# A macaron block on one core: first products of batches 2 to 5 moved from the loop to the front, the front's order changed, and the turn of xa put inside a value tile

## Chip, core and metric

The kernel runs on one core of a Trainium2 chip. The metric is the device time of one execution in microseconds (us), the median of several runs.

## What is computed

x has 8 batches of 512 tokens with 256 channels. All is float32. The first and the last stage are the same small FFN: eight adapters out of 32 are summed with weights into one 256 x 256 matrix. Between them stands a block with a recurrence over time (wkv) and a channel mix with 1024 hidden channels.

```python
def _L0_ffn_ref(x, W, b, ids, weights):
    out = jnp.einsum('k,kod,bsd->bso', weights, W[ids], x)
    return out + jnp.einsum('k,ko->o', weights, b[ids])

x = x + 0.5 * _L0_ffn_ref(_layernorm(x), ...)          # x1
x = x + _L0_attn_ref(_layernorm(x), ...)               # below
x = x + 0.5 * _L0_ffn_ref(_layernorm(x), ...)

# _L0_attn_ref
h = layernorm(x, ln1_g, ln1_b); hh = time_shift(h)
xk = h * tm_k + hh * (1 - tm_k)                        # xv, xr alike
k = xk @ Wk.T; v = xv @ Wv.T; sr = sigmoid(xr @ Wr.T)
x = x + (sr * wkv(time_decay, time_first, k, v)) @ Wo.T
h = layernorm(x, ln2_g, ln2_b); hh = time_shift(h)
xk = h * cm_k + hh * (1 - cm_k)                        # xr alike
kk = square(relu(xk @ Wck.T))
return x + sigmoid(xr @ Wcr.T) * (kk @ Wcv.T)
```

## The kernel before

Each of the engines (TensorE, VectorE, ScalarE, GpSimd, and SyncE for the transfers) has its own list of instructions, written out by hand. It works through its list in order and waits at semaphores for the others. Every batch passes through the stages below. Tiles lie with the tokens on the partitions (x1, xa, xs: 4 tiles of 128 tokens, 256 channels) or with the channels on the partitions (h1, xk, kk: 512 tokens in the free direction).

1. First product, y1 (L293, L271): `xt` (the batch of x, loaded with its channels on the partitions) times `ffn_t`, 16 matmuls in two banks of PSUM. The layer norm is applied behind it: VectorE takes the statistics of x (`stats_x`), GpSimd the inverse root `rstd_x` (L966) and adds the bias to x (`bias_to_x`, L986), and VectorE forms x1 = y1 * rstd_x + x (`add_first`, L696).
2. VectorE normalises x1 (`norm_first`, L716). TensorE turns it (`turn_x1`), ScalarE scales it into h1 (L473). VectorE forms the difference of h1 (L725) and the mixes xk, xv, xr (L734).
3. TensorE: products k, v, r (`front_k`, `front_v`, `front_r`, L277). VectorE scans and forms the gated wkv (L742 to L792), with exponentials on ScalarE and GpSimd. TensorE: output product (L326, L271).
4. VectorE adds it to xa (`add_output`, L798), takes statistics; GpSimd: inverse root `rstd_xa`; VectorE normalises (`norm_output`, L810). GpSimd sums xs = x1 + xa (`attention_sum`, L1016). TensorE turns xa (`turn_xa`), ScalarE forms h2 and the first part of the mix; VectorE finishes the mix xck (L818). ScalarE rounds it to its high part `xck_hi` (L503), VectorE takes the rest, `xck_lo` (L832).
5. TensorE: eight key blocks of the hidden layer, with the high and low parts of operand and weight (`channel_keys`, L340, L341, L344), a gate product (`channel_gate`), and four value tiles (`channel_values`, L362). ScalarE squares the relus. VectorE adds the values (`value_sum`, L840 and L843); GpSimd adds the bias of the last FFN (x2b, L986).
6. TensorE turns xs and makes the second product, and VectorE adds it (`add_second`, L866) for the store.

The lists are software pipelined. First comes a front for batch 0 (and the sums of batch 1). Then step e of a loop runs stages 5 and 6 of batch e and e - 1, stages 2 to 4 of batch f = e + 1, and stage 1 of batch f + 1. On TensorE a step is: keys with the turns of x1 and of xs between them, k, v, three keys, r, second product, gate, value tile 0, output product, first half of y1, value tile 1, second half of y1, turn of xa, value tiles 2 and 3. The next step begins with the keys, which want `xck_hi` and `xck_lo` of batch f.

PSUM is four pairs of banks. `PAIR` says which stage uses which pair, and `take` makes TensorE wait until the pair's last user has been read. In the front, TensorE runs matmuls on the identity (`warm(p, n)`, L254) that nobody reads, in its waits. `xt` has two buffers, x1 three. The SP queue loads in its own order: `load_x` (L199), `load_xt` (L206) and `store` (L213); a load into a buffer in use waits for its reader.

Of the kernel before, what the change touches and what calls it, by code (L numbers as in the profile page):

```python
# [10 lines left out]
P = 128  # L11
# [8 lines left out]
def build(nc, x, xt, ffn_w, ffn_b, ids, gates, vectors, wk, wv, wr, wo, wcr, wck, wcv, out):  # L20
# [4 lines left out]
    CH = C // P  # L25
# [6 lines left out]
    LAST = B - 1  # L32

    with ExitStack() as ctx:  # L34
# [38 lines left out]
        x2b = sb("x2b", [P, NT, C])  # L73
        kinds = ("x", "x1", "xa", "x2")
# [58 lines left out]
        thc_done, kvs_done = sem("thc_done"), sem("kvs_done")  # L133
# [33 lines left out]
        PAIR_BUT = {("y1", 1): 1, ("turn_x2", LAST): 2, ("y2", LAST): 1}  # L167
# [25 lines left out]
        def _(sp):  # L193
# [27 lines left out]
            load_xt(0)  # L221
            load_xt(1)
            load_x(1)
# [9 lines left out]
            load_xt(3)  # L233
            for e in range(B):
                load_x(e + 3)
                store(e - 1)
                load_xt(e + 4)
# [5 lines left out]
        def _(pe):  # L243
# [21 lines left out]
            def to_tokens(stage, src, w, signal, b, filled, part=range(BANKS)):  # L265
                for i in part:
                    take(pair_of(stage, b), i, signal, 2 * b + i + 1)
# [12 lines left out]
            def ffn_setup():  # L280
                pe.wait_ge(s_const, 4)
                warm(3, 36)
# [8 lines left out]
                last.then_inc(s_ffn_ps, 1)  # L291

            def first_product(f, part=range(BANKS)):  # L293
# [3 lines left out]
                to_tokens("y1", xt_sb[f % 2], ffn_t, x1_done, f, y1_ps, part)  # L297
# [55 lines left out]
            def channel_values(e, t):  # L353
# [3 lines left out]
                if t % TB == 0:  # L357
                    take(PAIR["kv"], i, kvs_done, 2 * e + i + 1)
                for n in range(HB):
# [4 lines left out]
                if t % TB == TB - 1:  # L364
                    last.then_inc(kv_ps, 1)
# [26 lines left out]
            warm(3, 8)  # L392
# [3 lines left out]
            pe.wait_ge(q_done, 2)  # L396
            warm(2, 47)
            output_product(0)
            pe.wait_ge(t1_done, 2)
            warm(3, 14)  # L400
            turn_xa(0)
            warm(3, 11)
            for e in range(B):
                f = e + 1

                early = (0, 1, 2) if has(e - 1) else (0, 1, 2, 3)
                late = (5, 6, 7) if has(e - 1) else (6, 7)
                channel_keys(e, early)
                if has(f):
                    turn_x1(f)  # L410
                if has(e - 1):
                    channel_keys(e, (3,))
                    turn_x2(e - 1)
                    channel_keys(e, (4,))
                else:
                    channel_keys(e, (4, 5))
# [3 lines left out]
                channel_keys(e, late)  # L420
# [8 lines left out]
                if has(f + 1):  # L429
                    first_product(f + 1, (0,))  # L430
                channel_values(e, 1)
                if has(f + 1):
                    first_product(f + 1, (1,))
                if has(f):
                    turn_xa(f)
                channel_values(e, 2)
# [657 lines left out]
```

## Time and profile before

| what | us |
|---|---|
| median of 3 runs (469.83 to 472.84) | 470.56 |
| the profiled execution, its own time | 470.55 |
| its span, first to last instruction | 468.8 |
| TensorE matmul busy in the span | 449.7 (96%) |
| VectorE busy | 385.6 (82%) |
| ScalarE busy | 255.4 (54%) |
| GpSimd busy | 156.3 (33%) |
| mean granted TensorE clock | 0.991 of full |

In the names of the profile PE is TensorE's matmul, PEld its weight load, DVE is VectorE, ACT ScalarE, POOL GpSimd and SP SyncE. A row of the timeline begins with the start and the length of a merged group of instructions; in brackets stands how long the engine had been idle ahead of it, and which instruction ended that. Buffer numbers are left out of the names: x is x1 there, and `work` is any tile of the recurrence. A busy PE is not a PE at its peak, since the ends of matmuls are modelled. The matmuls of the front include the ones on the identity.

### The profile page before, as it was taken

The page shows a single profiled execution, that of the slowest core. Times are in us where ns is not written, and L with a number is a line of the kernel's source. Part 1 is how long each engine was busy: PE and PEld are TensorE (multiplying, and loading weights), DVE is VectorE, ACT ScalarE, POOL GpSimd, SP SyncE. Part 2 cuts the span into 40 slices and gives each one's busy share as a digit, 9 for nine tenths or more (in the row PEclk, how much of TensorE's full clock was granted, in tenths as well). Part 3 has the DMA queues.
Part 4 walks back from the last instruction along what each step waited for, and adds up shares of the span by engine and source line. Part 5 has one row for each costly group of instructions (what it writes and reads, how often), then busy time and mean ns, then how long its engine had stood idle before and what let it go on. Part 6 is the DMA issues. An engine that isn't in the chain of part 4 may idle for free. (4 is left out here: it accounts for less than half of the span.)

```text
span 468.8 us, 5983 instructions
## 1 busy us (share of the span) xinstructions
PE 449.7 (96%) x2034; PEld 353.1 (75%) x2034; DVE 385.6 (82%) x796; ACT 255.4 (54%) x415; POOL 156.3 (33%) x126
## 2 busy tenths in 40 slices
PE   8959979999999999999999999999999999999996
PEld 8734966488857886788758886788668885778884
DVE  3778987998999798989899899979898999967124
ACT  1136637772878067924786167824794287816500
POOL 1344042415440543236240644035232444023010
PEclk9989999999999999999999999999999999999999
DMA  6950001002000020012001110010001000000101
GB/s 210 373 205 1 1 7 39 0 2 89 0 1 15 33 90 0 1 45 91 0 0 47 39 52 0 0 47 0 1 0 47 0 1 1 17 30 0 45 1 45
DMA packets 15952, 18.49 MB, mean 39 GB/s; under 512 B 1066, under 2 KB 13618, under 8 KB 15922
## 3 DMA queue, kind: packets, MB, share of 16 engines
q1 hardware_dynamic: 14522, 17.05, 10.4%
q10 hardware_dynamic: 1400, 1.07, 0.8%
q8 instruction: 16, 0.26, 0.2%
q14 instruction: 14, 0.11, 0.1%
HBM read 13.92 MB, written 4.19 MB: 39 GB/s over the span
## 5 line engine op out<-in xcount | busy, mean ns | idle before, releaser
L362 PE MATMUL pair<-wcv_sb,kk 128*128 128x256 f32 x512 | 114.3, 379 | 0.0
L362 PEld LDWEIGHTS pair<-wcv_sb,kk 128*128 128x128 f32 x512 | 96.7, 190 | 12.8
L966 POOL TENSOR_TENSOR rstd_x<-vare_x,nhalf 128x4 f32<-128x4 f32 (+1 forms) x25 | 30.2, 1207 | 102.0 <-DVE vare_x L654 101.1
L481 ACT ACTIVATE h<-pair,vec 128x512 f32<-128x512 f32 x16 | 11.6, 775 | 89.6 <-PE pair L262 89.6
L340 PE MATMUL pair<-xck_hi,wck_hi 128*128 128x512 f32 x128 | 55.6, 434 | 2.4 <-ACT xck_hi L503 1.3
L344 PE MATMUL pair<-xck_lo,wck_hi 128*128 128x512 f32 x128 | 50.2, 392 | 0.0
L341 PE MATMUL pair<-xck_hi,wck_lo 128*128 128x512 f32 x128 | 50.0, 390 | 0.0
L522 ACT ACTIVATE kk<-pair 128x512 f32<-128x512 f32 x64 | 37.9, 592 | 15.4 <-PE pair L344 13.5
L1009 POOL TENSOR_SCALAR work<-work,lowest 128x512 f32<-128x512 f32 x16 | 26.6, 1664 | 54.8 <-DVE work L745 54.8
L526 ACT ACTIVATE kk<-kk 128x512 f32<-128x512 f32 x64 | 38.8, 634 | 0.8
L986 POOL TENSOR_TENSOR x2b<-xs,bias_bc 128x512 f32<-128x512 f32 x15 | 19.2, 1280 | 52.1 <-DVE xs L843 52.1
L277 PE MATMUL pair<-xk,wk_sb 128*128 128x512 f32 x64 | 31.7, 642 | 4.3 <-issue 3.9
L340 PEld LDWEIGHTS pair<-xck_hi,wck_hi 128*128 128x128 f32 x128 | 24.1, 188 | 9.2 <-issue 3.2
L254 PE MATMUL pair<-ident 128*128 128x128 f32 x232 | 28.9, 288 | 2.1 <-POOL h L961 2.1
L254 PEld LDWEIGHTS pair<-ident 128*128 128x128 f32 x232 | 28.6, 205 | 2.7 <-POOL h L961 2.1
L271 PE MATMUL pair<-ffn_t,xt 128*128 128x256 f32 x128 | 29.9, 380 | 0.7 <-ACT ffn_t L458 0.7
L271 PE MATMUL pair<-ffn_t,x2t 128*128 128x256 f32 x128 | 29.2, 380 | 0.7 <-ACT x2t L552 0.7
L271 PEld LDWEIGHTS pair<-ffn_t,x2t 128*128 128x128 f32 x128 | 24.2, 190 | 6.8 <-issue 2.9
L277 PE MATMUL pair<-xr,wr_sb 128*128 128x512 f32 x64 | 28.8, 593 | 0.5 <-DVE xr L734 0.5
L271 PE MATMUL pair<-wo_sb,rwkv 128*128 128x256 f32 x128 | 29.1, 380 | 0.1
L271 PE MATMUL pair<-wcr_sb,xcr 128*128 128x256 f32 x128 | 28.9, 379 | 0.0
L277 PE MATMUL pair<-xv,wv_sb 128*128 128x512 f32 x64 | 28.8, 592 | 0.0
(115 smaller groups left out, 876.8 us busy)
## 6 DMA issues: line engine op xcount, KB each, us to landing
x<-in_x_dram SPq DMA_DIRECT2D x8, 512.0 KB, 4.7
xt<-in_xt_dram SPq DMA_DIRECT2D x8, 512.0 KB, 5.1
out_dram<-xs SPq DMA_DIRECT2D x16, 256.0 KB, 2.1
work<-in_ffn_w_dram ACTq DMA_DIRECT2D x4, 256.0 KB, 4.5
work<-in_ffn_w_dram SPq DMA_DIRECT2D x4, 256.0 KB, 4.6
kk<-in_wck_dram SPq DMA_DIRECT2D x1, 1024.0 KB, 9.0
wcv_sb<-in_wcv_dram SPq DMA_DIRECT2D x1, 1024.0 KB, 10.4
wk_sb<-in_wk_dram SPq DMA_DIRECT2D x1, 256.0 KB, 8.4
```

The costliest lines, as they stand in the source:

```text
L254: nc.tensor.matmul(pair[p][:, 0, 0:P], ident[:, :], ident[:, :], start=True, stop=True)
L271: last = nc.tensor.matmul(bank_of(stage, b, i)[:, t * C:(t + 1) * C], src[:, h, tok:tok + P], w[:, h, :], start=h == 0, stop=h == CH - 1)
L277: last = nc.tensor.matmul(bank, w[:, h, o * P:(o + 1) * P], src[:, h, :], start=h == 0, stop=h == CH - 1)
L340: nc.tensor.matmul(key_bank(n), wck_hi[:, h, cols], xck_hi[:, h, :], start=h == 0, stop=False)
L341: nc.tensor.matmul(key_bank(n), wck_lo[:, h, cols], xck_hi[:, h, :], start=False, stop=False)
L344: last = nc.tensor.matmul(key_bank(n), wck_hi[:, h, cols], xck_lo[:, h, :], start=False, stop=h == CH - 1)
L362: last = nc.tensor.matmul(bank_of("kv", e, i)[:, t % TB * C:(t % TB + 1) * C], kk[:, n, tok:tok + P], wcv_sb[:, n, :], start=n == 0, stop= ...
L522: nc.scalar.activation(kk[:, n, :], key_bank(n), ACT.Relu).then_inc(relu_done, 1)
L526: nc.scalar.activation(kk[:, n, :], kk[:, n, :], ACT.Square).then_inc(sq_done, 1)
L966: nc.gpsimd.tensor_tensor(dst, src, power, ALU.pow).then_inc(done, 1)
L986: nc.gpsimd.tensor_tensor(dst, tile, bias_bc[:, :].rearrange("p (a c) -> p a c", a=1).broadcast_to([P, tiles, C]), ALU.add).then_inc(done, 1)
L1009: nc.gpsimd.tensor_scalar(e_v[:, h, 0:T], q[:, h, 0:T], lowest[:, h:h + 1], None, ALU.max).then_inc(held_done, 1)
```

## The change

The first products of batches 2, 3, 4 and 5 (`EARLY`) leave the steps 0 to 3 and are computed in the front: 2 and 3 behind the r product of batch 0, 4 behind its output product, 5 behind its turn of xa. ScalarE copies them from PSUM to four new SBUF tiles, `y1s` (`keep_first`), and `add_first` reads them there. Their `xt` tiles are loaded in the front. Batches 6 and 7 stay as they were. In steps 0 to 3 the turn of xa stands in the middle of value tile 2 instead of ahead of it. In step 0 the turn of x1 stands behind three key blocks instead of four.

In the front, x(1) is loaded ahead of xt(1). The statistics and the sums of batch 1 come earlier on VectorE, the key weight's remainders ahead of the additions to xa, and all statistics of x1(1) ahead of the key mix. GpSimd adds the bias of batch 1 ahead of the inverses of batch 0, and forms xs(0) only when `xck_lo` is there. The warm matmuls change in number; those between r and the output product are replaced, but for 11, by the first products.

```diff
@@ -30,6 +30,8 @@
     LAST = B - 1
+    EARLY = range(2, 6)
@@ -71,6 +73,7 @@
         x2b = sb("x2b", [P, NT, C])
+        y1s = {b: sb(f"y1s_{b}", [P, NT, C]) for b in EARLY}
         kinds = ("x", "x1", "xa", "x2")
@@ -130,7 +133,7 @@
             sem(n) for n in ("xb_first", "xb_done", "x1_done", "normed1", "xa0_done", "xa2_done", "normeda", "xs_done", "x2_done", "x2b_done", "x3_done"))
-        thc_done, kvs_done = sem("thc_done"), sem("kvs_done")
+        thc_done, kvs_done, y1s_done = sem("thc_done"), sem("kvs_done"), sem("y1s_done")
@@ -164,7 +167,7 @@
         PAIR = {"turn_x1": 2, "turn_x2": 3, "y1": 2, "y2": 2, "k": 2, "v": 3, "r": 0, "cr": 1, "kv": 3, "o": 0, "turn_xa": 1}
-        PAIR_BUT = {("y1", 1): 1, ("turn_x2", LAST): 2, ("y2", LAST): 1}
+        PAIR_BUT = {("y1", 1): 1, ("y1", 3): 3, ("y1", 5): 3, ("turn_x2", LAST): 2, ("y2", LAST): 1}
@@ -219,8 +222,8 @@
             load_xt(0)
+            load_x(1)
             load_xt(1)
-            load_x(1)
             load_weight("wk", wk_sb[:, :, :], wk)
@@ -231,10 +234,12 @@
             load_xt(3)
+            load_xt(4)
+            load_xt(5)
             for e in range(B):
...
                 store(e - 1)
-                load_xt(e + 4)
+                load_xt(e + 6)
             store(LAST)
@@ -262,9 +267,9 @@
-            def to_tokens(stage, src, w, signal, b, filled, part=range(BANKS)):
+            def to_tokens(stage, src, w, signal, b, filled, part=range(BANKS), first=0):
                 for i in part:
-                    take(pair_of(stage, b), i, signal, 2 * b + i + 1)
+                    take(pair_of(stage, b), i, signal, 2 * (b - first) + i + 1)
                     for t in range(TB):
@@ -279,7 +284,7 @@
                 pe.wait_ge(s_const, 4)
-                warm(3, 36)
+                warm(3, 40)
                 pe.wait_ge(s_gate_rows, 1)
@@ -289,12 +294,17 @@
                 last.then_inc(s_ffn_ps, 1)
+                warm(3, 2)
...
                 pe.wait_ge(xt_loaded[f % 2], 16 * (f // 2 + 1))
-                to_tokens("y1", xt_sb[f % 2], ffn_t, x1_done, f, y1_ps, part)
+                if f in EARLY:
+                    to_tokens("y1", xt_sb[f % 2], ffn_t, y1s_done, f, y1_ps, part, first=EARLY[0])
+                else:
+                    to_tokens("y1", xt_sb[f % 2], ffn_t, x1_done, f, y1_ps, part)
@@ -350,18 +360,18 @@
-            def channel_values(e, t):
+            def channel_values(e, t, part=range(HB)):
                 i, tok = t // TB, t * P
...
                     pe.wait_ge(s_wcv, 1)
-                if t % TB == 0:
+                if t % TB == 0 and 0 in part:
                     take(PAIR["kv"], i, kvs_done, 2 * e + i + 1)
-                for n in range(HB):
+                for n in part:
                     if t == 0:
...
                                             start=n == 0, stop=n == HB - 1)
-                if t % TB == TB - 1:
+                if t % TB == TB - 1 and HB - 1 in part:
                     last.then_inc(kv_ps, 1)
@@ -389,35 +399,33 @@
             turn_x1(0)
-            warm(3, 8)
+            warm(3, 13)
             front_k(0)
...
             front_r(0)
-            pe.wait_ge(q_done, 2)
-            warm(2, 47)
+            first_product(2)
+            first_product(3)
+            pe.wait_ge(thr_done, 2)
+            warm(0, 11)
             output_product(0)
-            pe.wait_ge(t1_done, 2)
-            warm(3, 14)
+            first_product(4)
             turn_xa(0)
-            warm(3, 11)
+            first_product(5)
             for e in range(B):
...
-                early = (0, 1, 2) if has(e - 1) else (0, 1, 2, 3)
-                late = (5, 6, 7) if has(e - 1) else (6, 7)
-                channel_keys(e, early)
+                some = 5 if has(e - 1) else 6
+                channel_keys(e, (0, 1, 2))
                 if has(f):
                     turn_x1(f)
+                channel_keys(e, (3,))
                 if has(e - 1):
-                    channel_keys(e, (3,))
                     turn_x2(e - 1)
-                    channel_keys(e, (4,))
-                else:
-                    channel_keys(e, (4, 5))
+                channel_keys(e, range(4, some))
                 if has(f):
...
                     front_v(f)
-                channel_keys(e, late)
+                channel_keys(e, range(some, HB))
                 if has(f):
@@ -426,14 +434,17 @@
                     output_product(f)
-                if has(f + 1):
+                if has(f + 1) and f + 1 not in EARLY:
                     first_product(f + 1, (0,))
                 channel_values(e, 1)
-                if has(f + 1):
+                if has(f + 1) and f + 1 not in EARLY:
                     first_product(f + 1, (1,))
+                some = HB // 2 if f + 1 in EARLY else 0
+                channel_values(e, 2, range(some))
                 if has(f):
                     turn_xa(f)
-                channel_values(e, 2)
+                channel_values(e, 2, range(some, HB))
                 if e == LAST:
@@ -464,6 +475,11 @@
                 nc.scalar.activation(wcv_sb[:, :, :], wcv_sb[:, :, :], ACT.Copy, scale=0.5).then_inc(s_wcv, 1)
+            def keep_first(b):
+                for i in range(BANKS):
+                    act.wait_ge(y1_ps, 2 * b + i + 1)
+                    nc.scalar.activation(tok_bank(y1s[b], i), bank3(bank_of("y1", b, i)), ACT.Copy).then_inc(y1s_done, 1)
@@ -588,11 +604,15 @@
             residual_of(0)
+            keep_first(2)
+            keep_first(3)
             setup_wcv()
+            keep_first(4)
             h2_of(0)
...
             past_cr(0)
+            keep_first(5)
             for e in range(B):
@@ -691,9 +711,14 @@
                 for i in part:
-                    dve.wait_ge(y1_ps, 2 * b + i + 1)
+                    if b in EARLY:
+                        dve.wait_ge(y1s_done, 2 * (b - EARLY[0]) + i + 1)
+                        product = tok_bank(y1s[b], i)
+                    else:
+                        dve.wait_ge(y1_ps, 2 * b + i + 1)
+                        product = bank3(bank_of("y1", b, i))
                     for t in range(i * TB, (i + 1) * TB):
-                        last = nc.vector.scalar_tensor_tensor(tile[:, t, :], bank3(bank_of("y1", b, i))[:, t % TB, :], rstd_x[b % 2][:, t:t + 1],
+                        last = nc.vector.scalar_tensor_tensor(tile[:, t, :], product[:, t % TB, :], rstd_x[b % 2][:, t:t + 1],
                                                               tile[:, t, :], ALU.mult, ALU.add)
@@ -875,12 +900,13 @@
             bias_to_first()
+            stats_x(1)
             add_first(0, (0,))
...
             norm_first(0)
-            stats_x(1)
+            add_first(1)
             mixes(0)
@@ -892,17 +918,15 @@
             wkv_gated(0)
-            add_first(1)
+            key_weight_rest(0)
+            key_weight_rest(1)
             add_output(0)
-            key_weight_rest(0)
             norm_output(0)
-            key_weight_rest(1)
-            stats_x1(1, (0,))
+            stats_x1(1)
             mix_ck(0)
             key_input_rest(0)
-            stats_x1(1, (1,))
+            norm_first(1)
             mix_cr(0)
-            norm_first(1)
             for e in range(B):
@@ -1023,15 +1047,17 @@
             inverse_x(0)
-            first_inverses(0)
             inverse_x(1)
...
             bias_to_x(1)
+            first_inverses(0)
             pool.wait_ge(s_decay, 2)
...
             inverse_std("xa", 0)
+            first_inverses(1)
+            pool.wait_ge(xck_lo_done, CH)
             attention_sum(0)
-            first_inverses(1)
             for e in range(B):
...
                 if has(e - 1):
```

## Rows read from the trace of the kernel before

**Rows 1.** Waits of PE from 110 to 420 us: total, times, longest.

```profile
PE pair L262 <- DVE norma L810: 0.7, 1, 0.7
```

**Rows 2.** Timeline of PE, step 1 into step 2: start, length, engine, line, operation.

```profile
153.39 3.62 PE L271 MATMUL pair<-wo_sb,rwkv 128*128 128x256 f32 x16
156.84 1.89 PE L271 MATMUL pair<-ffn_t,xt 128*128 128x256 f32 x8
...
171.34 0.58 PE L340 MATMUL pair<-xck_hi,wck_hi 128*128 128x512 f32 x1
...
180.17 3.59 PE L277 MATMUL pair<-xk,wk_sb 128*128 128x512 f32 x8
```

**Rows 3.** Timeline of DVE, POOL and ACT behind that output product.

```profile
159.07 0.88 DVE L696 SCALAR_TENSOR_TENSOR x<-pair,rstd_x,x 128x256 f32<-128x256 f32 x2
159.22 1.02 POOL L966 TENSOR_TENSOR rstd_xa<-vare_xa,nhalf 128x4 f32<-128x4 f32 x1 [2.03 <-DVE vare_xa L654]
...
161.79 2.36 POOL L1016 TENSOR_TENSOR xs<-x,xa 128x1024 f32<-128x1024 f32 x1 [1.55 <-issue]
162.22 0.69 DVE L840 SCALAR_TENSOR_TENSOR thc<-thc,pair 128x512 f32<-128x512 f32 x1 [0.57 <-PE pair L362]
162.94 1.75 DVE L843 TENSOR_TENSOR xs<-xs,thc 128x512 f32<-128x512 f32 x1
...
164.77 1.27 POOL L986 TENSOR_TENSOR x2b<-xs,bias_bc 128x512 f32<-128x512 f32 x1 [0.62 <-DVE xs L843]
165.40 0.86 DVE L696 SCALAR_TENSOR_TENSOR x<-pair,rstd_x,x 128x256 f32<-128x256 f32 x2
...
168.22 1.41 DVE L818 SCALAR_TENSOR_TENSOR xck<-h,vec,xck 128x512 f32<-128x512 f32 x2
...
169.00 1.30 ACT L503 ACTIVATE xck_hi<-xck 128x512 fp32r<-128x512 f32 x2 [1.94 <-DVE xck L818]
...
177.16 1.36 DVE L725 TENSOR_TENSOR xr<-h 128x512 f32<-128x512 f32 x2 [0.80 <-ACT h L473]
```

**Rows 4.** Timeline of the front, all engines.

```profile
28.14 3.49 DVE L734 SCALAR_TENSOR_TENSOR xk<-xr,vec,h 128x512 f32<-128x512 f32 x2
28.48 2.60 POOL L986 TENSOR_TENSOR x<-x,bias_bc 128x1024 f32<-128x1024 f32 x1
...
31.73 6.45 PE L277 MATMUL pair<-xk,wk_sb 128*128 128x512 f32 x8 [3.92 <-issue]
...
45.58 10.66 PE L254 MATMUL pair<-ident 128*128 128x128 f32 x94
...
61.83 1.22 DVE L822 TENSOR_TENSOR wck_lo<-kk,wck_hi 128x1024 fp32r<-128x1024 f32 x1
62.01 1.94 POOL L966 TENSOR_TENSOR rstd_xa<-vare_xa,nhalf 128x4 f32<-128x4 f32 x1 [17.58 <-DVE vare_xa L654]
...
64.86 1.43 PE L262 MATMUL pair<-ident,norma 128*128 128x128 f32 x8 [1.95 <-DVE norma L810]
...
67.99 1.95 DVE L818 SCALAR_TENSOR_TENSOR xck<-h,vec,xck 128x512 f32<-128x512 f32 x2 [0.83 <-ACT xck L489]
...
70.08 0.47 PE L340 MATMUL pair<-xck_hi,wck_hi 128*128 128x512 f32 x1 [1.33 <-ACT xck_hi L503]
```

**Rows 5.** Timeline of step 0, from the difference of h1 to k.

```profile
77.31 1.36 DVE L725 TENSOR_TENSOR xr<-h 128x512 f32<-128x512 f32 x2 [1.63 <-ACT h L473]
...
80.05 3.70 PE L277 MATMUL pair<-xk,wk_sb 128*128 128x512 f32 x8 [0.42 <-DVE xk L734]
```

**Rows 6.** Stretches: busy PE, PEld, DVE, ACT, POOL (counts), granted clock, DMA share, GB/s.

```profile
31.50:37.00 5.50, 5.27 (x7) 2.20 (x8) 2.80 (x5) 0.00 (x0) 0.00 (x0) 0.50 0.00 0
...
62.80:64.90 2.10, 0.15 (x3) 0.07 (x2) 1.17 (x4) 0.00 (x0) 1.15 (x1) 1.00 0.00 0
```

**Rows 7.** Timeline of step 6, which has no first product: a mix beside POOL.

```profile
422.55 1.27 POOL L986 TENSOR_TENSOR x2b<-xs,bias_bc 128x512 f32<-128x512 f32 x1 [0.63 <-DVE xs L843]
...
423.18 1.86 DVE L818 SCALAR_TENSOR_TENSOR xck<-h,vec,xck 128x512 f32<-128x512 f32 x2
```

## Prediction

> **What bounds the kernel now.** The profiled execution took 470.55 us, its span is 468.8 us, and the median of the three runs shown is 470.56 us. The profiled execution is an ordinary one, so I sum against 470.55 us. I read the waits first, in the stretch from 110 to 420 us, which holds steps 1 to 6. TensorE (PE) waits there once, for 0.7 us [rows 1]. That looks like a kernel in which every microsecond taken from PE is gained. The timeline corrects this, and it is the second view. A step is a ring of two engines. From the k product to the output product PE has no gap. From the output product to the next k product VectorE (DVE) must add, normalise, mix and form xk, and it has almost no gap either. Behind the output product of 153.39 us, DVE waits 0.57 us for a value tile at 162.22 and 0.80 us for h1 at 177.16, and nothing else above 0.4 us [rows 2, 3]. A product taken out of PE behind the output product is worth only what DVE can follow.
>
> Third I read the front (0 to 70 us). It is one serial chain. xk is mixed in 3.49 us while GpSimd (POOL) adds the bias to x [rows 4]. PE, idle 3.92 us, then does the k product in 6.45 us, where the same product of batch 1 takes 3.70 us [rows 4, 5]. The granted clock says why: it is 0.50 (1.2 instead of 2.4 GHz) from 31.5 to 37 us [rows 6].
>
> **The front, first part.** Statistics of x(1) move ahead of the first sums: 4 statistics, 4 aggregations and an addition. They stand where DVE waited for PE, and delay the first sum by some 0.5 us at most. POOL adds the bias in that time, before the inverses of batch 0, instead of at 28.48. The four sums of batch 1 (0.88 us a pair, as at 159.07 in [rows 3]) move ahead of the mixes and fill the time in which DVE would wait for h1. I estimate that the xk mix, at 28.14 before, starts at 28.45, since some 0.3 us of these delays stay. It no longer meets POOL and takes 1.41 us, as the mix at 168.22 does [rows 3]. It ends at 29.86, and k starts 0.13 behind it at 29.99 instead of 31.73: 1.74 us gained. A warm matmul takes 10.66 / 47 = 0.23 us [rows 4]; the 13, behind the turn, end near 29.3, so PE idles about 0.7 us instead of 3.92. The clock should hold, and the product shortens from 6.45 to 3.70, which passes through the two scans of k as about 2.65 us. Gained so far 4.4 us. The four extra warm products and the swap of the loads of x(1) and xt(1) end under that 0.5 us and cost nothing more.
>
> **The front, second part.** From the r product to the keys PE ran warm matmuls. Four first products (3.46 us each, as the output product does from 153.39 to 156.84) take their places: batches 2 and 3 after r, 4 after the output product, 5 after the first turn of xa. The one of batch 3 must wait until DVE has read v in pair 3. There is room for that: the two products need 6.9 us of the 10.66 us that the 47 warm matmuls at 45.58 filled [rows 4]. ScalarE (ACT) makes eight copies, which I put at the 0.65 us of its pass at 169.00 (1.30 for two) [rows 3]. Six stand in its long wait for the turn of xa. The last two stand ahead of the first relu of step 0 and delay the third key block by an estimated 0.9 us; the turn of x1 one block earlier, and the end of the old 0.42 us wait ahead of k at 80.05, pay for it. Net nothing; uncovered, it would be 0.9 us. The transfers of xt(4) and xt(5) are issued behind the products of batches 2 and 3, that is ahead of the output product, and are wanted behind it. On the SP queue no store is behind their waits.
>
> The two remainders of the key weight (1.22 us each) leave the place behind the statistics of xa [rows 4]. There one ran beside POOL's inverse root, which took 1.94 us against 1.02 us in [rows 3]: 0.92 us gained, less an estimated 0.1 by which they now delay the additions to xa. The sum x1 + xa on POOL now waits for the key input's remainder, so the mix of xck (1.95 us at 67.99 in [rows 4], 1.41 in [rows 3]) loses its collision: keys 5.22 us after the turn of xa before [rows 4], 4.7 after (64.86 to 67.99, then 0.78 + 0.65 + 0.1 as in [rows 3]), and turn and first product of batch 5 (1.3 + 3.46) just fit. Front: 4.4 + 0.85 + 0.5 = 5.7 us.
>
> **The steps.** In steps 0 to 3 PE drops 3.46 us. Four times that is 13.8 us, which I do not believe. Follow the step [rows 2, 3]:
> - The inverse root of xa (POOL, 159.22) runs beside the sum at 159.07. That sum read PSUM and x1; now it reads two SBUF tiles. By the collision in [rows 4] the root waits for the sum that is running: 159.07 + 0.44 - 159.22, about 0.25 us late.
> - The value sum no longer waits its 0.57 us. But its second half (162.94, 1.75 us instead of 0.69) ends 0.54 us behind POOL's sum xs (161.79 + 2.36 = 164.15), which starts when the normalisation is done and does not ask for PE. Nothing gained.
> - The second pair of sums (165.40) meets POOL's bias sum of x2b (164.77 to 166.04). With PSUM as a source they took 0.86. With two SBUF sources they should behave as the mix at 423.18, which took 1.86 instead of 1.41 beside such a sum [rows 7]: finished about 0.3 + 0.4 us behind its end, at 166.73 instead of 166.26, 0.47 us late.
> - So the mix of xck starts at 168.22 + 0.25 + 0.47 = 168.94. Its high part starts 0.78 us behind it (169.00) and takes 0.65 for the first half; with some 0.1 us to PE the keys start at 170.5. PE is through its values at 171.34 - 3.46, plus the 0.2 us by which a turn that splits a tile may wait, at 168.1: a gap of 2.4 us that was not there.
> - DVE reaches the difference of h1 at 177.16 - 0.80 + 0.72 = 177.08, and k follows 2.74 us later: 179.82 against 180.17. That is 0.3 us per step; of the keys' lead (0.85 us) the rest is lost again at k. The turn inside the third value tile lets the normalisation (done 161.7 + 0.25) arrive in time, PE coming there at 156.84 + 3.45 + 1.73 = 162.02; without it PE would wait, but not DVE.
>
> The ends of the unknown: 0 to 0.72 us of delay from the two collisions, thus a gain of 0.3 to 1.05 us a step. I take 0.3, because both pairs of tiles lie in SBUF as in [rows 7]. Four steps: 1.2 us. Steps 4 to 7 are unchanged. The Trainium skill (SBUF — State Buffer, Who interferes with whom) says that a DVE instruction with two SBUF inputs and a GpSimd instruction that reads SBUF exclude each other, and that the second to issue blocks until the first is done. The 1.86 and 1.75 us above agree.
>
> **The clock in the new gaps.** PE stood 3.92 us and lost its clock [rows 4, 6]. In a gap of 1.95 us ahead of 64.86 it kept it [rows 4, 6]. 2.4 us lies between. A fall costs nothing at least, and at most the 5.5 us at half speed of [rows 6], 2.75 us, less 0.5 us by which k waits for DVE anyway: 2.2 us. I take 1.2 us for one, and none or one in the four gaps: 0.6 us.
>
> **Sum.** 470.55 - 5.7 - 1.2 + 0.6 = 464.2 us. Chance 0.55, own range 462.5 to 466.
>
> **Rivals.**
> 1. The sums do not collide (DVE reads y1s without a loss): 1.05 us a step, 470.55 - 5.7 - 4.2 = 460.7. The copies being in SBUF speaks against it. 0.11.
> 2. PE alone sets the step, and all 13.8 us come: 451. The single wait of PE in 310 us speaks for it [rows 1], DVE's chain against. 0.06.
> 3. The front does less than it says: the clock still falls ahead of k, because the start of the chain is late and the gap stays long. The 2.65 us stay away: 466.9, or less if more is late. 0.10.
> 4. The clock falls in two or three of the new gaps: 466 to 468.5. 0.10.
> 5. The other side. The clock falls ahead of the keys in all four steps and stays down as long as in the front: 4 x 2.2 = 8.8 us lost, 470.55 - 6.9 + 8.8 = 472.5. It outweighs the gain from 1.7 us a gap. For it speaks that 2.4 us is longer than any gap here that kept the clock, against it that DVE, not PE, sets k. 0.08. The Trainium skill (TensorE: Matmul & The Clock Gate, Part 1) has the same two levels and lets idleness bring the lower; it tells this case no price.
>
> **How the numbers follow.** The range 460.5 to 468.5 takes in rivals 1, 3 and 4, and leaves out 2, 5 and little else. A measurement of this kernel tells about 1% (4.7 us) from no change, a limit at 465.85: faster has the forecast and rivals 1 and 2, less the forecast's upper edge, 0.67. Slower by over 1% needs more than rival 5: 0.04. The rest, 0.29, is within 1%.
>
> **What would show it.** The k product of batch 0 should start near 30 us at clock 1.0 and take 3.7 us. The first keys should start near 64.3. In steps 1 to 4 the keys should wait about 2.4 us for xck_hi, the k products 0.3 to 0.8 us for xk, and the steps should be 51.2 us apart, as against 51.5. The second pair of sums should measure 1.3 us instead of 0.86, and the root of xa 1.25 instead of 1.02. PE steps of 48.1 us without a wait would make the prediction wrong, as would a clock of 0.5 behind each gap.

## The result, and the profile after

| kernel | median, us | single executions | ratio to before, 95% interval |
|---|---|---|---|
| before | 470.19 | 469.08 to 472.84 | 1 |
| changed | 464.44 | 462.45 to 465.04 | 0.9859 [0.9815, 0.9903] |
| changed, run again | 463.57 | 462.60 to 466.44 | 0.9874 [0.9848, 0.99] |

The ratios are those on record, from executions side by side; the quotient of the first two medians would be 0.9878. The forecast was 464.2 us. The profiled execution took 462.45 us (span 460.7), 8.1 us less than the one before. The first thing to read is where PE waits now. The waits of the changed kernel, PE from 100 to 280 us (total, times, longest; that stretch holds the ends of steps 0 to 3):

```profile
PE pair L350 <- ACT xck_hi L519: 8.8, 4, 2.2
```

Before, PE never waited there [rows 1]. The timeline of PE in the changed kernel shows the front and one of those four gaps (L267 turns, L282 is k, L276 a first or output product, L350 the keys):

```profile
29.60 3.67 PE L282 MATMUL pair<-xk,wk_sb 128*128 128x512 f32 x8 [0.39 <-issue]
...
48.38 2.62 PE L259 MATMUL pair<-ident 128*128 128x128 f32 x22
51.42 3.69 PE L276 MATMUL pair<-wo_sb,rwkv 128*128 128x256 f32 x16 [0.42 <-issue]
54.95 3.62 PE L276 MATMUL pair<-ffn_t,xt 128*128 128x256 f32 x16
59.29 1.43 PE L267 MATMUL pair<-ident,norma 128*128 128x128 f32 x8 [0.72 <-DVE norma L835]
60.55 3.62 PE L276 MATMUL pair<-ffn_t,xt 128*128 128x256 f32 x16
63.97 0.47 PE L350 MATMUL pair<-xck_hi,wck_hi 128*128 128x512 f32 x1
...
163.61 0.47 PE L350 MATMUL pair<-xck_hi,wck_hi 128*128 128x512 f32 x1 [2.19 <-ACT xck_hi L519]
...
172.79 3.70 PE L282 MATMUL pair<-xk,wk_sb 128*128 128x512 f32 x8
```

Against [rows 4] the first k product starts 2.13 us earlier and takes 3.67 instead of 6.45 us, and the keys come at 63.97 instead of 70.08. The granted clock, with the stretch in front, the busy times of PE, PEld, DVE, ACT and POOL (and their counts) behind it, then the clock, explains the length. The kernel before stood at 0.50 in that place [rows 6]:

```profile
24.90:29.60 4.70, 4.17 (x34) 3.77 (x35) 4.70 (x11) 3.60 (x4) 0.45 (x3) 1.00 0.89 330
29.60:34.00 4.40, 4.40 (x11) 2.01 (x12) 3.50 (x5) 0.43 (x2) 0.19 (x1) 1.00 0.01 3
```

The timeline of DVE and POOL in the changed kernel, behind the output product of step 1. It answers to [rows 3] (L721 is L696 there, L990 is L966, L835 the normalisation, L1040 is L1016, L868 is L843, L1010 is L986, L843 is L818, L750 is L725):

```profile
152.25 0.88 DVE L721 SCALAR_TENSOR_TENSOR x<-y1s,rstd_x,x 128x256 f32<-128x256 f32 x2
152.39 1.22 POOL L990 TENSOR_TENSOR rstd_xa<-vare_xa,nhalf 128x4 f32<-128x4 f32 x1 [2.08 <-DVE vare_xa L674]
...
153.65 1.38 DVE L835 TENSOR_SCALAR norma<-xa,mv_xa,rstd_xa 128x256 f32<-128x256 f32 x4 [0.52 <-POOL rstd_xa L990]
...
155.16 2.36 POOL L1040 TENSOR_TENSOR xs<-x,xa 128x1024 f32<-128x1024 f32 x1 [1.55 <-issue]
...
155.66 2.41 DVE L868 TENSOR_TENSOR xs<-xs,thc 128x512 f32<-128x512 f32 x1
...
158.14 1.27 POOL L1010 TENSOR_TENSOR x2b<-xs,bias_bc 128x512 f32<-128x512 f32 x1 [0.63 <-DVE xs L868]
158.77 1.32 DVE L721 SCALAR_TENSOR_TENSOR x<-y1s,rstd_x,x 128x256 f32<-128x256 f32 x2
...
162.06 1.41 DVE L843 SCALAR_TENSOR_TENSOR xck<-h,vec,xck 128x512 f32<-128x512 f32 x2
...
170.11 1.29 DVE L750 TENSOR_TENSOR xr<-h 128x512 f32<-128x512 f32 x2
```

The value sum (L868) came 0.5 us behind the start of POOL's sum and took 2.41 instead of 1.75 us: what DVE no longer waited for the value tile it waits inside the instruction. The root took 1.22 instead of 1.02, the second pair of sums 1.32 instead of 0.86. L750 follows without a wait. Up to L843 this is all DVE's chain; PE reaches the end of its value tiles in the meantime and stands for the last 2.2 us ahead of the keys.

That is one execution, and the front shifts as a whole from one to the next. In the trace of the changed kernel run again, the first k product starts almost 1 us later and takes the same time:

```profile
30.57 3.67 PE L282 MATMUL pair<-xk,wk_sb 128*128 128x512 f32 x8 [0.39 <-issue]
```

The k products show where the time went. They start at 73.69, 121.65, 172.79, 223.90 and 275.05 us in the changed kernel, and at 80.05, 128.62, 180.17, 231.72 and 283.27 us before. The lead is 6.4 us at the end of the front, and grows by 0.6, 0.4, 0.4 and 0.4 us over steps 0 to 3 to 8.2 us. PE had dropped 3.46 us in each of them. From there on it stays. In the second trace the lead is 5.4 us at the end of the front (74.69) and 7.2 us behind step 3 (276.04).

### The profile page after: what moved, and what is told of

Its sections match the earlier page's. It is cut to its first block and busy times, and to the rows that moved or that the text cites. A ratio compares the mean times of both kernels' runs of the same rounds, so it can differ in the third digit from the quotient of the medians.

```text
span 460.7 us, 5788 instructions
## 1 busy us (share of the span) xinstructions
PE 438.1 (95%) x1934; PEld 339.4 (74%) x1934; DVE 388.1 (84%) x796; ACT 259.0 (56%) x423; POOL 156.8 (34%) x126
## 5 line engine op out<-in xcount | busy, mean ns | idle before, releaser
L990 POOL TENSOR_TENSOR rstd_x<-vare_x,nhalf 128x4 f32<-128x4 f32 (+1 forms) x25 | 31.3, 1250 | 101.6 <-DVE vare_x L674 100.7
L350 PE MATMUL pair<-xck_hi,wck_hi 128*128 128x512 f32 x128 | 55.3, 432 | 9.9 <-ACT xck_hi L519 8.8
L350 PEld LDWEIGHTS pair<-xck_hi,wck_hi 128*128 128x128 f32 x128 | 24.1, 188 | 18.1 <-issue 12.1
L1010 POOL TENSOR_TENSOR x2b<-xs,bias_bc 128x512 f32<-128x512 f32 x15 | 19.2, 1281 | 52.1 <-DVE xs L868 52.1
L282 PE MATMUL pair<-xk,wk_sb 128*128 128x512 f32 x64 | 29.3, 600 | 0.8 <-issue 0.4
L276 PE MATMUL pair<-ffn_t,x2t 128*128 128x256 f32 x128 | 29.2, 380 | 0.7 <-ACT x2t L568 0.7
L276 PE MATMUL pair<-ffn_t,xt 128*128 128x256 f32 x128 | 29.3, 381 | 0.6 <-DVE work L792 0.3
L276 PE MATMUL pair<-wo_sb,rwkv 128*128 128x256 f32 x128 | 29.1, 381 | 0.6 <-issue 0.4
L282 PE MATMUL pair<-xr,wr_sb 128*128 128x512 f32 x64 | 28.8, 593 | 0.7 <-DVE xr L759 0.7
L354 PEld LDWEIGHTS pair<-xck_lo,wck_hi 128*128 128x128 f32 x128 | 24.0, 188 | 7.4 <-DVE xck_lo L857 1.8
L276 PEld LDWEIGHTS pair<-ffn_t,x2t 128*128 128x128 f32 x128 | 24.3, 190 | 6.7 <-issue 2.9
L276 PE MATMUL pair<-wcr_sb,xcr 128*128 128x256 f32 x128 | 28.9, 379 | 0.0
L282 PE MATMUL pair<-xv,wv_sb 128*128 128x512 f32 x64 | 28.8, 592 | 0.0
L351 PEld LDWEIGHTS pair<-xck_hi,wck_lo 128*128 128x128 f32 x128 | 24.1, 189 | 5.6 <-issue 1.7
```

Source lines behind the costliest of these rows:

```text
L276: last = nc.tensor.matmul(bank_of(stage, b, i)[:, t * C:(t + 1) * C], src[:, h, tok:tok + P], w[:, h, :], start=h == 0, stop=h == CH - 1)
L282: last = nc.tensor.matmul(bank, w[:, h, o * P:(o + 1) * P], src[:, h, :], start=h == 0, stop=h == CH - 1)
L350: nc.tensor.matmul(key_bank(n), wck_hi[:, h, cols], xck_hi[:, h, :], start=h == 0, stop=False)
L351: nc.tensor.matmul(key_bank(n), wck_lo[:, h, cols], xck_hi[:, h, :], start=False, stop=False)
L354: last = nc.tensor.matmul(key_bank(n), wck_hi[:, h, cols], xck_lo[:, h, :], start=False, stop=h == CH - 1)
L990: nc.gpsimd.tensor_tensor(dst, src, power, ALU.pow).then_inc(done, 1)
```

## The experiments

The theory on trial: a step is as long as the slower of PE's work and a chain that runs from the output product over DVE to the next k product. The front gives the larger part of the gain, since it is one chain and had a low clock in it. The rival is what the change looks like: PE is busy 96% of the time, and products that leave the steps give the gain.

**The two halves.** The first kernel keeps the front's order and puts the products back into the steps:

```diff
-    EARLY = range(2, 6)
+    EARLY = range(0)
...
-            first_product(2)
-            first_product(3)
-            pe.wait_ge(thr_done, 2)
-            warm(0, 11)
+            pe.wait_ge(q_done, 2)
+            warm(2, 43)
             output_product(0)
-            first_product(4)
+            pe.wait_ge(t1_done, 2)
+            warm(3, 14)
             turn_xa(0)
-            first_product(5)
+            warm(3, 11)
...
```

> The changed kernel with the first products of batches 2 to 5 back in the steps 0 to 3 (turn of xa behind them) and warm matmuls in their places in the front; all other changes of the front stay. My theory: the front's order makes the larger part of the gain and the four products only what DVE can follow in the steps. The traces give 6.4 us up to the k product of step 0 and 0.4 us for each of four steps, so this should lose about 1.7 us of the 5.8 us: ratio to the kernel before 0.990 (465.6 us), no gaps ahead of the keys, steps of 51.5 us. The rival, that taking 13.8 us off PE makes the gain and the front's order little: ratio near 0.999 (469.5 us).

Measured: 464.24 us, ratio 0.9876 [0.9857, 0.9895]. The first k product starts at 29.73 us and takes 3.67, steps are 51.55 us long (k at 173.58 and 225.13), and PE has no gap in them. I expected 465.6; the front alone gave 1.4 us more than that and as much as the whole change did.

The second kernel keeps the products in the front and restores the front's old order on DVE, POOL and SP, and the old warm matmuls:

```diff
+            load_xt(1)
             load_x(1)
-            load_xt(1)
...
-            warm(3, 13)
+            warm(3, 8)
...
-            stats_x(1)                    # stood ahead of add_first(0)
...
-            add_first(1)                  # stood ahead of mixes(0)
+            stats_x(1)
...
+            add_first(1)                  # now ahead of add_output(0)
...
```

> The other half: the products of batches 2 to 5 in the front, the copies and the turn inside value tile 2, but the order of the front on DVE, POOL and the SP queue and the warm matmuls ahead of the first k product as before. My theory: about 1.7 us for the steps, and the first k product again at 31.7 us with 6.4 us at the low clock: ratio 0.996 (468.4 us), gaps of 2.2 us ahead of the keys. The rival: 0.988 or lower (464.5 us).

Measured: 469.05 us, ratio 0.9977 [0.996, 0.9995]. The products alone are worth 0.2%, about 1 us. The k product of batch 0 is again the slow one, and the gaps ahead of the keys are there. Timeline of PE in this kernel, then its stretches around the first of the gaps:

```profile
31.76 6.51 PE L282 MATMUL pair<-xk,wk_sb 128*128 128x512 f32 x8 [3.92 <-issue]
...
119.44 0.76 PE L349 MATMUL pair<-xck_hi,wck_hi 128*128 128x512 f32 x1 [2.23 <-ACT xck_hi L518]
```

```profile
117.00:119.40 2.40, 0.21 (x1) 0.00 (x0) 2.24 (x10) 0.70 (x2) 1.34 (x1) 1.00 0.00 0
119.40:123.00 3.60, 3.56 (x9) 2.83 (x10) 3.60 (x8) 2.35 (x4) 1.90 (x4) 0.53 0.02 5
123.00:126.00 3.00, 3.00 (x19) 2.52 (x18) 2.86 (x10) 2.47 (x6) 1.29 (x1) 1.00 0.00 0
```

So such a gap can cost the clock: the 0.53 over 3.6 us is half speed for about 3.4 us. In the front of the kernel before, the stretch at half speed lasted 6.8 us (30.5 to 37.3). The other three gaps of the same execution (2.20 to 2.21 us) kept the clock.

**The turn of xa back ahead of value tile 2.**

```diff
-                some = HB // 2 if f + 1 in EARLY else 0
+                some = 0
```

> The changed kernel with the turn of xa ahead of value tile 2 in steps 0 to 3 as before. My theory: the keys wait for DVE anyway, so PE waits about 1 us at the turn and 1.2 instead of 2.2 us at the keys, and the time stays within 0.3 us of the changed kernel (0.987, 464.2 us), or a little lower if the smaller gaps keep the clock up. The rival, that this wait adds to the time: 4 x 1 us more, 0.996.

Measured: 462.73 us, ratio 0.9841 [0.9823, 0.986]. PE's waits from 100 to 280 us in this kernel:

```profile
PE pair L267 <- DVE norma L835: 3.6, 4, 0.9
PE pair L350 <- ACT xck_hi L519: 3.0, 4, 0.8
```

The 2.2 us of a gap are now 0.9 at the turn and 0.8 at the keys, and the steps are still 51.1 us long (k at 173.24 and 224.37). The part of the change that was to let PE reach the turn without a wait is worth nothing in itself: DVE sets the keys. The four executions took 462.53 to 463.12 us, at mean clocks of 0.998 to 1.0. The changed kernel scattered from 462.45 to 466.44 us. So two gaps of under 1 us kept the clock here where one of 2.2 us sometimes lost it, and splitting the value tile may have cost 1 us or so; the intervals of the two ratios overlap, so that is not shown.

**The clock term of the front by itself.**

```diff
             turn_x1(0)
-            warm(3, 13)
             front_k(0)
```

> The changed kernel without the 13 warm matmuls between the first turn of x1 and the first k product (they compute nothing). It prices the clock term of the front by itself. PE then stands for about 3.4 us. My theory: the granted clock falls as it did before the change, the k product takes 5 to 6.5 us instead of 3.7, and the time rises by 1.5 to 2.7 us (0.991 to 0.993 of the kernel before). The rival, that the gain of the front came from the earlier start of k alone: no change against the changed kernel (0.987).

Measured: 466.04 us, ratio 0.9909 [0.989, 0.9927]. Timeline of PE and the stretches in this kernel:

```profile
29.67 5.83 PE L282 MATMUL pair<-xk,wk_sb 128*128 128x512 f32 x8 [3.29 <-DVE xk L758]
```

```profile
28.00:34.00 6.00, 4.33 (x5) 1.85 (x6) 3.33 (x6) 1.84 (x2) 0.00 (x0) 0.50 0.16 62
```

The k product starts where it did, and takes 5.83 instead of 3.67 us. Of that 2.16 us, about all comes through to the end: 466.04 us is 1.6 us above the first median of the changed kernel and 2.5 above the second. The comparison can't be finer, since the gaps ahead of the keys lose the clock in some executions of both kernels (in this profiled one twice, behind 114.45 and 166.81 us). Thirteen matmuls that nobody reads are worth some 2 us.

**Work put into the gap.** The changed kernel, run again beside the next three:

> The changed kernel itself, run beside the next three for their comparison. Its first four times ran from 462.45 us (mean granted clock 0.998) to 465.04 us (0.995). My theory: the clock falls in some executions in a gap of 2.2 us ahead of the keys, at about 2 us a fall: ratio 0.987, with times on two levels some 2 us apart. The rival, one level with noise: times spread evenly.

Its executions, time and mean granted clock, with those of the first comparison:

| mean clock | times, us |
|---|---|
| 0.998 to 0.999 | 462.45, 462.60, 463.46 |
| 0.995 | 463.37, 463.55, 463.60, 464.38, 464.49 |
| 0.992 | 465.04, 465.48 |
| 0.988 | 466.44 |

There are four levels rather than two, about 1.2 us apart on average ((466.44 - 462.84) / 3). A step of 0.0035 in the mean clock over 461 us is 3.2 us at half speed, about the length that the stretch above shows. I read the levels as none, one, two or three falls in the four gaps. Mostly there was one, 12 in these 11 executions. That is argued from the mean clocks. The two traces of this kernel (0.998 and 0.999) have no fall; those of its relatives have one (the second kernel), two (the one without the 13 warm matmuls) and two (the one below with the bias sum moved, mean clock 0.992), each of 3.4 us. PE and a stretch in the last of these:

```profile
163.10 0.47 PE L350 MATMUL pair<-xck_hi,wck_hi 128*128 128x512 f32 x1 [1.75 <-ACT xck_hi L519]
```

```profile
163.00:167.00 4.00, 3.90 (x10) 2.91 (x11) 4.00 (x9) 3.08 (x5) 1.96 (x4) 0.63 0.00 0
```

Even a gap of 1.75 us can cost the clock, then, and a fall can be priced by the k products of that trace: the two steps with one are 52.0 us long, the one between them 50.5. In the kernel without the 13 warm matmuls such a step is 52.2 us long, against 51.1 without a fall. A fall costs 1.0 to 1.5 us.

By this reading it is plain why the front alone did as well as the whole change. The executions of the changed kernel without a fall have a mean of 462.84 us, 1.4 us below the 464.24 of the front alone, which has no gaps. The products' leaving gives about that much and mostly loses it to the clock in the gaps that it opens.

The next kernel fills those gaps:

```diff
                 channel_values(e, 3)
+                if f + 1 in EARLY:
+                    pe.wait_ge(*((x3_done, 2 * e) if e > 0 else (q_done, 4)))
+                    warm(2, 9)
```

> The changed kernel with 9 warm matmuls (2.05 us by the trace, nobody reads them) behind value tile 3 in steps 0 to 3, in the gap in which PE waits 2.2 us for the keys' operand. Two questions. First, whether PE has slack there: if DVE sets the step, as I hold, 8 us of added PE work cost nothing; if PE sets it, the time rises by up to 8 us (0.987 to 1.004). Second, whether the clock falls in that gap: then the filled kernel stays on the lower level, 462.4 us, ratio 0.983, with a clock of 0.998 in all executions.

Measured: 462.99 us, ratio 0.9849 [0.983, 0.9869]; four executions from 462.56 to 463.74 us, three of them at a clock of 1.0. Timeline of PE in this kernel, at the end of step 1:

```profile
161.58 2.17 PE L259 MATMUL pair<-ident 128*128 128x128 f32 x18
163.95 0.47 PE L350 MATMUL pair<-xck_hi,wck_hi 128*128 128x512 f32 x1 [0.20 <-ACT xck_hi L522]
```

More than eight microseconds on PE (four times 2.17), and the time does not rise. PE is not what bounds steps 0 to 3. The scatter is smaller as well, 1.2 us over four executions, though one of them still had a clock of 0.996 (463.74 us), which I had not expected.

**One collision less.** POOL's bias sum for the first half of x2b goes behind the held exponents of the next step, where DVE has room:

```diff
...
                     hold_exponents(f)
+                if has(e - 1) and f in EARLY:
+                    bias_to_x2(e - 1, 0)
...
-                bias_to_x2(e, 0)
+                if f + 1 not in EARLY:
+                    bias_to_x2(e, 0)
```

> The changed kernel with POOL's bias sum of the first half of x2b moved, in steps 0 to 3, behind the held exponents of the next step. It takes away the collision with the second pair of sums from y1s (1.32 us, 0.86 without). My theory: DVE sets the step, so four times 0.46 us come off: 1.8 us less than the changed kernel, ratio 0.983, second pair at 0.9 us. The rival, that the collision lies beside the path: no change.

Measured: 462.55 us, ratio 0.9824 [0.98, 0.9847], 1.0 us below the changed kernel beside it, with 460.75 us in the one execution at a clock of 1.0. Timeline of DVE in this kernel:

```profile
108.03 0.86 DVE L721 SCALAR_TENSOR_TENSOR x<-y1s,rstd_x,x 128x256 f32<-128x256 f32 x2
```

The pair of sums is back from 1.32 to 0.86 us, and the gap ahead of the keys shrinks from 2.2 to 1.75 us, so the 0.46 us come off DVE's chain: step 0 takes 47.50 us from k to k, against 47.96. The medians show less than the 1.8 us expected. Their intervals overlap, and clock falls scatter both (this kernel's profiled execution has two). The one execution at a clock of 1.0 lies 2.1 us below the mean of the changed kernel's without a fall (460.75 against 462.84), which fits the 1.8 us but is a single one.

**DVE's order.** On top of the last one, the sums and statistics of x1 go ahead of the value sum in steps 0 to 3. PE's list is that of the changed kernel:

```diff
+                soon = f + 1 in EARLY
                 if has(f + 1):
-                    add_first(f + 1, (0,))
+                    add_first(f + 1, (0, 1) if soon else (0,))
                 if has(f):
                     norm_output(f)
+                if soon:
+                    stats_x1(f + 1)
                 value_sum(e, 0)
                 value_stats(e, 0)
-                if has(f + 1):
+                if has(f + 1) and not soon:
                     add_first(f + 1, (1,))
                     stats_x1(f + 1)
```

> On top of the last one, in steps 0 to 3: all four sums of x1 from y1s ahead of the normalisation of xa, and the statistics of x1 between it and the value sum. So single-source statistics stand under POOL's sum xs (2.36 us), where the value sum was blocked (2.41 us instead of 0.69). PE's work is the same. My theory (DVE's chain from the output product to k sets the step): the mix of xck starts about 2.6 us earlier, the gap ahead of the keys closes, k comes 2.6 us earlier per step, and the time falls by about 10 us below the changed kernel: 453 us, ratio 0.963. The rival (PE and the products set it, DVE's order is free): within 1 us of the changed kernel. If only the collision counts and something else is late next, between: 458 us.

Measured: 453.93 us, ratio 0.9656 [0.9638, 0.9674]. It beats both kernels. The timeline of DVE, POOL and PE in it, step 1:

```profile
150.52 1.67 DVE L721 SCALAR_TENSOR_TENSOR x<-y1s,rstd_x,x 128x256 f32<-128x256 f32 x4
...
153.40 1.40 DVE L661 BATCH_NORM_STATS2 bn_x<-x 128x6 f32<-128x256 f32 x4
...
153.62 2.37 POOL L1043 TENSOR_TENSOR xs<-x,xa 128x1024 f32<-128x1024 f32 x1 [1.74 <-issue]
...
155.30 0.71 DVE L673 TENSOR_SCALAR both<-mv_x 128x4 f32<-128x4 f32 x1
...
156.70 0.69 DVE L868 TENSOR_TENSOR xs<-xs,thc 128x512 f32<-128x512 f32 x1
...
158.10 1.40 DVE L843 SCALAR_TENSOR_TENSOR xck<-h,vec,xck 128x512 f32<-128x512 f32 x2
...
168.82 3.70 PE L282 MATMUL pair<-xk,wk_sb 128*128 128x512 f32 x8
```

The statistics read one tile and run at their old 1.40 us beside POOL's sum, and the value sum comes when POOL is through: 0.69 instead of 2.41 us. The gap ahead of the keys is gone, and the k products are 48.9 us apart (119.91, 168.82, 217.67) instead of 51.1. The 2.23 us of a step can be followed in the two timelines, from the last row on the statistics of xa to the mix of xck (152.14 to 162.06, and 150.41 to 158.10 us). The value sum gives 1.72, DVE's wait for POOL's root (0.52 ahead of L835), which the second pair of sums now fills, 0.52, and that pair without its collision 0.53. Of this 0.54 is lost again, since `both` (L673) now lasts 0.71 instead of 0.17 us, until POOL's sum is through. So the value sum is the largest term, but not the only one. PE and the other engines in this step (busy times as above):

```profile
119.91:168.82 48.91, 48.81 (x208) 37.05 (x208) 46.04 (x98) 30.99 (x52) 20.06 (x14) 1.00 0.10 33
```

PE is busy in 48.8 of the 48.9 us, so it is now a bound as well, although k still starts as DVE's xk ends. (By subtraction PE's work would be 51.55 - 3.46 = 48.1 us; no run says where the other 0.7 us come from.) Most of the 13.8 us that left PE were here: 9.0 us by the k products over steps 0 to 3, 9.6 us by the medians, come with an order on another engine and one bias sum on POOL.

Two controls separate what made it. First the same kernel with POOL's bias sum in its old place:

```diff
-                if f + 1 not in EARLY:
-                    bias_to_x2(e, 0)
+                bias_to_x2(e, 0)
...
```

> The reordered kernel (sums and statistics of x1 ahead of the value sum) with POOL's bias sum of x2b in its old place. It separates the order from the collision. Now the mix of xck should meet that bias sum and take 1.86 us instead of 1.41. My theory: the order carries 7.8 of the 9.6 us, and the place of the bias sum 0.45 us a step: 455.7 us, ratio 0.9695. The rival, that the bias sum's place is half of it or more: 459 us.

Measured: 455.83 us, ratio 0.9698 [0.967, 0.9726]. The mix of xck takes 1.85 us, as expected. The order carries 7.7 us (463.57 to 455.83; 7.1 by the k products over steps 0 to 3), the place of the bias sum 1.9. Then DVE's order with the products in the steps, both halves behind the output product, and the front as in the first experiment:

```diff
+                soon = f + 1 in range(2, 6)
                 if has(f + 1):
-                    first_product(f + 1, (0,))
+                    first_product(f + 1, (0, 1) if soon else (0,))
                 channel_values(e, 1)
...
```

> The same order on DVE (all sums and statistics of x1 ahead of the value sum in steps 0 to 3), but with the first products in the steps, both halves behind the output product, and the front as in the run with the front alone. My theory: a step is the slower of PE's work (51.5 us with the products) and DVE's chain, so the order alone gives nothing without the products' leaving: 464.2 us as with the front alone, ratio 0.9876, no waits of PE in the steps. The rival, that DVE's order gives its 10 us by itself: 455 us, ratio 0.968.

Measured: 464.17 us, ratio 0.9877 [0.9849, 0.9905], the same as the front alone (0.9876). PE has no waits in the steps. So the order gives nothing without the products' leaving, the leaving gives little without the order, and together they give 8.3 us (464.17 to 455.83), or 10 with the bias sum moved.

## Why the prediction was right, point by point

- **The front** was put at 5.7 us. The k product of batch 1 came 6.4 us earlier in one trace and 5.4 in the other, and the front alone measured 5.8 us (0.9876 of 470). The start of k was forecast at 29.99; the ten traces with this front's order have it between 29.60 and 30.57 us, so its 0.4 us in the first trace can't be told from the scatter. The sums of batch 0 came later about as I let them (normalisation of x1 at 24.00 against 23.71 us). But from there to the mix of xk it took 4.09 instead of 4.43 us in both traces of the changed kernel, because DVE's four sums (1.65 us) are shorter than the statistics and aggregations that had stood there; that I had not counted. From the start of k to the k product of batch 1 it took 44.09 instead of 48.32 us, 4.2 us gained against 4.0 forecast (2.65 + 0.85 + 0.5; the 0.85 should be 0.82 by its own terms). The product took 3.67 us at full clock, as forecast, and the keys came at 63.97 against 64.3. The clock's part was confirmed by taking the warm matmuls away: a gap of 3.29 us where the old one had 3.92, a product of 5.83 where the old one had 6.45, and 1.6 to 2.5 us more in the medians, where I had put 2.65.
- **The copies on ACT** were put at nothing net. The k product follows the keys by 9.72 us against 9.97 before [rows 4, 5], so they were covered. They were not free: in the kernel with the front alone, which has no copies, it is 9.50 us. The third key block came 0.2 us late (3.25 us behind the first instead of 3.06 there), where I had given it 0.9.
- **The steps** were put at 0.3 us of the 3.46 us each. Measured 0.4 (0.6 in step 0). The gap was forecast at 2.4 us and is 2.2, the wait for xk ahead of k at 0.3 to 0.8 and is about 0.3, the second pair of sums at 1.3 and is 1.32, the root at 1.25 and is 1.22, the distance of the k products at 51.2 and is 51.1. The step's reason was shown three ways: more than 8 us of added PE work cost nothing, a turn at which PE waits 0.9 us costs nothing, and 9.6 us come from DVE's and POOL's order with PE's list untouched.
- **The value sum** that was said to gain nothing from its earlier start took 2.41 instead of 1.75 us and ended 0.55 us behind POOL's sum, as before.
- **The clock in the gaps** was put at half a fall of 1.2 us, between 0 and 2.2. A fall costs 1.0 to 1.5 us, but by the levels there was about one in an execution, not half of one. Rival 5, four falls as long as in the front, was too dark in the number and in the length: 3.4 us at half speed in a gap against 6.8 in the front. Why the lengths differ, and why some of these gaps lose the clock and others do not, is open. Rival 4, two or three falls, is what 3 of the 11 executions had.
- **The sum** came out 0.2 us from the first median and 0.6 us from the second, partly by luck, since two errors cancel. Without falls the forecast is 463.6 us and the measurement 462.8; the falls cost about 1.2 us (the mean of the 11 executions is 464.1) where I had put 0.6.
- **The rivals.** PE alone as the bound (451 us) fell with the filled gap. Sums without a collision (460.7) fell with the 1.32 us, and the kernel that takes the collision away shows what it was worth. The clock before the first k product held.

I had named the collision of the value sum with POOL's sum and called it "nothing gained". I did not ask what a step would be worth in which other work stands there. That was the larger number of this case: 7.7 us for DVE's order, against 1.9 us for the moved products by the k products of the trace (8.2 - 6.4), most of which, by the levels above, the clock took back.

## What to carry to other kernels

Work taken off the engine that looks full is worth what the next chain can follow. Sum that chain between its two meetings with the full engine before counting the gain, and then look for the instruction in it that is long because of a neighbour. In this front, a stand of TensorE of over 3 us cost more than the wait, since the product behind it ran at half clock (5.83 instead of 3.67 us). And a product taken out of a dense stretch can open a gap that costs the clock: look whether a few matmuls that nobody reads, or a wait split in two, keep it.

## What the runs showed of the hardware beyond that

A DVE instruction that reads one float32 SBUF tile can be held up by POOL as well. Timeline of DVE and POOL in the changed kernel, step 0, where the normalisation of x1(1) meets POOL's sum xs, which the change had moved away from the mix:

```profile
65.13 3.46 DVE L741 TENSOR_SCALAR norm<-x,mv_x,rboth 128x256 f32<-128x256 f32 x4
65.29 2.50 POOL L1040 TENSOR_TENSOR xs<-x,xa 128x1024 f32<-128x1024 f32 x1
```

Alone these four take 1.38 us (in the kernel before, at 74.30 us). Four statistics, which read one tile too, take 1.40 us beside POOL's sum (at 153.40 us in the reordered kernel) and 1.40 without it (at 59.70 in this one). The collision that the change took from the mix (0.54 us) thus returned as 2.1 us on the normalisation, where it cost nothing, because the k product of batch 1 started without a wait. The Trainium skill (SBUF — State Buffer, Who interferes with whom) counts `tensor_scalar` among the operations that can use both ports and so contend; the row agrees, 3.46 against 1.38 us. The forecast had watched only the instructions with two tiles.
